# A two-layer cross-attention and expert network on one core: first experts on tokens sorted by expert, one batch behind the other, query and key stacks written from SBUF to SBUF

## The reference

```python
x = x + L0_xattn(layernorm(x), ctx)   # 16 heads of 8, softmax(q k / sqrt(8)) v, biases
x = x + L0_ffn(layernorm(x))          # 8 experts, 128 -> 512 -> 128, gelu, one expert a token
x = x + L1_xattn(layernorm(x), ctx)   # 16 query heads on 8 key heads, inputs quantised to 8 bit,
                                      # weights to -1, 0, 1; layernorm and requantising before Wo
x = x + L1_ffn(layernorm(x))          # 15 experts 128 -> 128 -> 128, relu, top 3 of a softmax,
                                      # and one shared expert
# L0_ffn:
idx = argmax(softmax(logits)); score = gates[idx]
h = gelu(x @ w1[e] + b1[e]); y = h @ w2[e] + b2[e]     # for every e
out = y[idx] * score
```

## Time and profile before

| what | value |
|---|---|
| runs, us | 273.32, 275.46, 277.76 (median 275.46) |
| span of the profiled execution, first to last instruction | 272.9 us |
| instructions | 4924 |
| PE busy | 225.1 us, 82% |
| DVE busy | 172.3 us, 63% |
| ACT busy | 140.1 us, 51% |
| POOL busy | 65.5 us, 24% |

### The profile page before, as it was taken

One profiled execution on the slowest core, in us unless ns is written; L12 is line 12 of the kernel. 1 busy time (PEld: TensorE's weight loads), 2 busy tenths in 40 slices (PEclk: granted clock), 3 DMA queues, 4 the chain that ended last, 5 costly groups with the idle time before them and its releaser, 6 DMA issues.

```text
span 272.9 us, 4924 instructions
## 1 busy us (share of the span) xinstructions
PE 225.1 (82%) x1700; PEld 141.5 (52%) x1700; DVE 172.3 (63%) x486; ACT 140.1 (51%) x329; POOL 65.5 (24%) x123
## 2 busy tenths in 40 slices
PE   2444697799898899999999985776997779979994
PEld 1323143434343379898899862222333233877893
DVE  7770697898793033232563588794898832887864
ACT  3411025688787763534454443723886386454551
POOL 6792059652295200100110000700000111111000
PEclk9999997999999999999999999577899798999999
DMA  6079013820058500000002000292000000000000
GB/s 176 13 133 222 13 30 107 251 53 17 3 164 214 155 2 0 1 4 0 2 0 68 21 0 1 70 269 59 0 4 1 2 0 2 1 0 2 19 4 19
DMA packets 10888, 14.36 MB, mean 53 GB/s; under 512 B 2698, under 2 KB 8512, under 8 KB 10672
## 3 DMA queue, kind: packets, MB, share of 16 engines
q1 hardware_dynamic: 7568, 6.92, 9.4%
q0 software_dynamic: 2528, 6.60, 9.2%
q10 hardware_dynamic: 768, 0.53, 0.7%
HBM read 11.73 MB, written 2.23 MB: 51 GB/s over the span
## 4 chain that ended last, share of the span: by engine, by line
PE 56%; DVE 14%; DMA 9%; POOL 6%; ACT 5%; SPq 5%; issue 4%; DVEq 0%; ACTq 0%; POOLq 0%
PE SB L1467 10%; PE OB L1402 9%; PE OB L1481 5%; DVE mx L1038 5%; PE SB L1513 5%; PE SA L1481 5%; PE SB L1382 4%; PE SA L1352 4%; PE SA L1524 4%; SPq L510 4%; DMA K<-k_dram 2%; ACT prob L798 2%; DMA k_dram<-kp 2%; DMA q_dram<-qp 2%; DMA wgn<-in_L_ffn_wg_dram 1%
## 5 line engine op out<-in xcount | busy, mean ns | idle before, releaser
L1038 DVE TENSOR_REDUCE mx<-SA 128x1 bf16<-128x512 f32 x128 | 79.9, 683 | 20.2 <-PE SA L1352 19.7
L798 ACT ACTIVATE prob<-SB 128x512 f32<-128x512 f32 x128 | 67.7, 598 | 25.9 <-PE SB L1382 25.3
L1352 PE MATMUL SA<-K,Q 64*128 64x512 bf16 x128 | 36.3, 441 | 14.3 <-DMA K<-k_dram 6.0
L1402 PE MATMUL OB<-prob,V 128*32 128x256 f32 x512 | 42.2, 416 | 1.7 <-ACT oT L806 1.5
L859 ACT ACTIVATE prob<-SB,b1T 128x256 f32<-128x256 f32 x64 | 26.7, 470 | 30.1 <-PE SB L1467 30.1
L1382 PE MATMUL SB<-Q,K 64*128 64x256 bf16 x256 | 31.9, 295 | 3.8 <-ACT prob L798 2.5
L633 POOL TENSOR_SCALAR vareps<-mv 128x2 f32<-128x2 f32 x10 | 1.9, 190 | 135.9 <-DVE mv L929 135.8
L1467 PE MATMUL SB<-hT,w1s 128*128 128x256 f32 x128 | 33.3, 385 | 0.6 <-ACT prob L859 0.6
L1352 PEld LDWEIGHTS SA<-K,Q 64*128 64x128 bf16 x128 | 9.4, 96 | 34.8 <-DVE mx L1038 19.2
L1467 PEld LDWEIGHTS SB<-hT,w1s 128*128 128x128 f32 x128 | 22.1, 190 | 3.8 <-ACT prob L859 1.5
L1382 PEld LDWEIGHTS SB<-Q,K 64*128 64x128 bf16 x256 | 12.0, 98 | 23.1 <-ACT prob L798 11.0
(11 more groups left out here) (249 smaller groups left out, 285.3 us busy)
## 6 DMA issues: line engine op xcount, KB each, us to landing
w1s<-in_L_ffn_w_dram POOLq DMA_DIRECT2D x8, 256.0 KB, 4.1
w2s<-in_L_ffn_w_dram POOLq DMA_DIRECT2D x8, 256.0 KB, 4.7
K<-k_dram SPq DMA_DIRECT2D x12, 128.0 KB, 5.2
Q<-q_dram SPq DMA_DIRECT2D x18, 64.0 KB, 2.2
e1w<-in_L_ffn_eW_dram POOLq DMA_DIRECT2D x1, 960.0 KB, 6.4
e2w<-in_L_ffn_eW_dram POOLq DMA_DIRECT2D x1, 960.0 KB, 7.9
q_dram<-qp SPq DMA_DIRECT2D x12, 64.0 KB, 1.7
k_dram<-kp SPq DMA_DIRECT2D x6, 128.0 KB, 1.8
```

What stands on the lines that cost most here:

```text
L798: act.activation(prob[:, g % 2, 2 * (i % 2) + a, 2 * u:2 * u + 2, :].rearrange("p k q -> p (k q)"), SB[n % 3][:, :], ACT.Exp).then_inc(s_e ...
L1038: dve.tensor_reduce(mx[:, g % 2, r, 2 * a + i // 2:2 * a + i // 2 + 1], SA[SCORE_BANK[n]][:, :], AX, ALU.max).then_inc(s_sa_max, 1)
L1352: pe.matmul(SA[SCORE_BANK[u]][:, :], Q[n][rows, b, p, r * P:(r + 1) * P], K[n][rows, b, key_group(n, p), :], start=True, stop=True).then_i ...
L1402: last = pe.matmul(OB[32 * j:32 * j + 32, 0:NQ], V[n][:, b, kt, first:first + 32], prob[:, gg % 2, j, kt, :], start=(kt == 0), stop=(kt == ...
```

## The change

- First experts. After the gate of a batch, count0, slots0 and tiles0 give every token a slot among 16 tiles of 32 slots, so that each tile holds tokens of one expert. gather0 multiplies the tokens by a 0/1 matrix (perm), 512 columns; permT0 makes its transpose. For each of four chunks of four tiles: weights0 copies each tile's expert weights (128x1024 f32) on POOL, at an address read from the computed table, into one of two chunk buffers; h0 is a bias product and four products of 32 rows by 512 columns side by side; ACT applies gelu to 128x512; gelT0 turns it; y0 is a bias product and sixteen products of 32 rows by 128 columns; scatter0 brings the outputs back to token order.
- Order. One list, written out. Batch 0's first experts follow layer 0's attention; then batch 0's queries of layer 1 and the scores of group 8; batch 1's first experts lie between the steps of groups 9 to 11; then batch 1's queries and the scores of group 12; batch 0's second experts lie between the steps of groups 14 and 15; batch 1's output turn to its last norm follow; then batch 1's second experts.
- Maxima. DVE turns them in 32x32 blocks; PE's two products and the copy are gone, and SP issues four transfers instead of two.
- Stacks. The parts go from kp and qp straight into K and Q, six transfers each, with no DRAM between them. Layer 1 uses layer 0's memory again.
- Banks. Two SA banks instead of three; two X banks in turn for all else, and the attention's banks once it has ended.

```diff
+elif kind == "weights0":                                            (gpsimd)
+    _, b, c = step
+    if c == 0:
+        pool.wait_ge(s_eid, b + 1)
+    before = nth(*step) - 3
+    if before >= 0:
+        pool.wait_ge(*xfull(("y0", before // CHUNKS, before % CHUNKS)))
+    for j in range(4):
+        place = pool.value_load(eid[0:1, b, 4 * c + j:4 * c + j + 1], min_val=0, max_val=E0 - 1)
+        pool.tensor_copy(wq[:, c % 2, j, :], w0s[:, bass.ds(place, 1), :].rearrange("p o f -> p (o f)")).then_inc(s_wq, 1)
...
+elif kind == "h0":                                                  (scalar)
+    act.activation(gel[:, c % 2, :], xbank(step)[:, :], ACT.Gelu).then_inc(xdone(step), 1)
...
+elif kind == "h0":                                                  (tensor)
+    pe.matmul(bank[:, :], owners[:, 4 * c:4 * c + 4, :].rearrange("e j s -> e (j s)"), b1s[:, :], start=True, stop=False)
+    for j in range(4):
+        pe.wait_ge(s_wq, 4 * nth("weights0", b, c) - 3 + j)
+        at = c * P + 32 * j
+        last = pe.matmul(bank[32 * j:32 * j + 32, :], xs[:, at:at + 32], wq[:, c % 2, j, 0:F0], start=False, stop=True)
...
+elif kind == "y0":                                                  (tensor)
+    pe.wait_ge(*xread("gelT0", b, c))
+    pe.matmul(bank[:, 0:D], owners[:, 4 * c:4 * c + 4, :].rearrange("e j s -> e (j s)"), b2r[:, :], start=True, stop=False)
+    for k in range(FC):
+        for j in range(4):
+            last = pe.matmul(bank[32 * j:32 * j + 32, 0:D], gelT[:, c % 2, k * P + 32 * j:k * P + 32 * j + 32],
+                             wq[:, c % 2, j, at:at + D], start=False, stop=(k == FC - 1))
...
+dve.transpose(nm[:, g % 2, :, :, :].rearrange("p x c r -> p x r c"), mx[:, g % 2, :, :, :]).then_inc(s_nm, 1)
...
-sp.dma_start(dram[part].rearrange("e s c -> (e s) c"), parts[:, part, :]).then_inc(written[part], 16)
+engine.dma_start(K[n][b][row:P:8, :, :], kp[0:P // (n + 1), u, part, :]).then_inc(s_kst[n][b], 16)
...
 SCHEDULE (batch 0's experts; the handovers)
+('weights0', 0, 0), ('weights0', 0, 1), ('h0', 0, 0), ('gelT0', 0, 0), ('h0', 0, 1), ('y0', 0, 0), ('weights0', 0, 2),
+('gelT0', 0, 1), ('h0', 0, 2), ('y0', 0, 1), ('weights0', 0, 3), ('out_turn', 0, 1, 0), ('gelT0', 0, 2), ...
+('scatter0', 0), ('turn', 'f0', 1), ('stats', 'q1', 0), ('red0', 1), ('norm', 'q1', 0), ('logits0', 1), ('quant', 'q1', 0),
+('gate_exp0', 1), ('turn', 'q1', 0), ('count0', 1), ('qproj', 1, 0), ('slots0', 1), ('qstack', 1, 0), ('scores', 8, 0),
+('scores', 8, 1), ('scores', 8, 2), ('scores', 8, 3), ('max_rows', 8), ('scores', 9, 0), ('scores', 9, 1),
+('scores', 9, 2), ('exp', 8, 0), ...
```

More of the change, by code:

```diff
@@ L237 @@
-SCHEDULE = build_schedule()
-def between(step):
-    at = SCHEDULE.index(step)
-    return any(SCHEDULE.index(("exp", 8 * n, 0)) < at < SCHEDULE.index(("exp", 8 * n + 7, 3)) for n in range(2))
-X_WANT = {
-    "ctxq_turn": lambda s: [s[1]], "kproj": lambda s: [0], "vproj": lambda s: [1] if s[1] else [],
-    "turn": lambda s: [int(s[1] == "q0")],
-    "qproj": lambda s: [1], "bias_turn": lambda s: [0], "w1_measure": lambda s: [1],
-    "w1_turn": lambda s: [1], "wg_turn": lambda s: [0], "out_turn": lambda s: [s[3]], "att_turn": lambda s: [0],
-    "out_proj": lambda s: [1], "red0": lambda s: [0], "logits0": lambda s: [1],
-    "max_rows": lambda s: [0], "bias0": lambda s: [0, 1], "logits1": lambda s: [1], "bias1": lambda s: [0, 1],
-}
@@ new lines, with place_banks @@
+X_USES = {"ctxq_turn": 1, "kproj": 1, "vproj": 1, "turn": 1, "qproj": 1, "bias_turn": 1, "w1_measure": 1, "w1_turn": 1,
+          "wg_turn": 1, "out_turn": 1, "att_turn": 1, "out_proj": 1, "red0": 1, "logits0": 1, "count0": 1, "slots0": 1,
+          "tiles0": 1, "gather0": 1, "permT0": 1, "h0": 1, "gelT0": 1, "y0": 1, "scatter0": 1, "logits1": 1, "bias1": 2,
+          "hidden1": 1, "output1": 1}
+def place_banks():
+    banks, counts, last, used = {}, {}, {}, [0] * (3 + NSA + NSB)
+    for at, step in enumerate(SCHEDULE):
+        uses = X_USES.get(step[0], 0)
+        if not uses:
+            continue
+        free = [0, 1]
+        if at > SCHEDULE.index(("scores", 15, 3)):
+            free += list(range(2, 2 + NSA))
+        if at > SCHEDULE.index(("exp", 15, 3)):
+            free += list(range(2 + NSA, 2 + NSA + NSB))
+        if at > SCHEDULE.index(("values", 15, 3)):
+            free += [2 + NSA + NSB]
+        banks[step] = []
+        for k in range(uses):
+            bank = min(free, key=lambda x: last.get(x, -1))
+            last[bank] = at + 0.5 * k
+            used[bank] += 1
+            banks[step].append(bank)
+            counts[step, k] = used[bank]
+    return banks, counts
@@ L289 @@
+X_BANKS, X_COUNT = place_banks()
+OUTPUTS_BEFORE = {("bias1", b): sum(s[0] == "output1" for s in SCHEDULE[:SCHEDULE.index(("bias1", b))]) for b in range(B)}
 ORDER = {}
@@ L487, in xread, with turned, columns, buffer_free @@
             return x_read[X_BANKS[step][k]], X_COUNT[step, k]
+        def turned(bank, stage):
+            return bank[:, 0:NQ] if stage[0] != "q" else bank[:, 0:NQ].rearrange("d (r p) -> d p r", r=R)
+        def columns(stage, b):
+            return hT[:, b, :] if stage[0] != "q" else hT[:, b, :].rearrange("d (p r) -> d p r", r=R)
+        def buffer_free(engine, step):
+            kind, b = step[:2]
+            if b and kind == "gather0":
+                engine.wait_ge(*xfull(("h0", b - 1, CHUNKS - 1)))
+            elif b and kind in ("permT0", "y0"):
+                engine.wait_ge(*xfull(("scatter0", b - 1)))
         def split_group(g):
@@ L818, in _ @@
                     last.then_inc(s_sq, 1)
-                elif kind in ("turn", "att_turn", "red0", "bias0", "bias1") and step in ON_SCALAR:
+                elif kind in ("turn", "att_turn", "red0", "bias1", "gather0", "permT0", "gelT0", "y0") and step in ON_SCALAR:
                     b = step[-1]
@@ L822, in _ @@
                     if kind == "turn":
-                        last = act.activation(hT[:, b, :], xbank(step)[:, 0:NQ], ACT.Copy)
+                        last = act.activation(columns(step[1], b), turned(xbank(step), step[1]), ACT.Copy)
                     elif kind == "att_turn" and step[1] == 0:
@@ L1308, in _ @@
                     _, n, b = step
+                    fill(step)
                     if n == 0:
@@ L1443, in _ @@
                     last.then_inc(xfull(step)[0], 1)
-                elif kind == "bias0":
+                elif kind == "count0":
+                    b = step[1]
+                    fill(step)
+                    pe.wait_ge(s_place, 4)
+                    pe.wait_ge(s_cw, CW_AT["logits0", b])
+                    for r in range(R):
+                        last = pe.matmul(xbank(step)[0:E0, 0:1], oh_b[:, r, :], ones_b[:, 0:1], start=(r == 0), stop=(r == R - 1))
+                    last.then_inc(xfull(step)[0], 1)
+                elif kind == "slots0":
                     b = step[1]
```

847 lines of the change are left out of this document (362 added, 485 removed), and 33 rows, old and new, of tables (ON_SCALAR, SCHEDULE).

## The result

The changed kernel takes 338.5 us (median of 4 runs, 336.42 to 340.32), the kernel before 276.4 in the same comparison (273.32 to 277.76): a ratio of 1.229 with a 95% interval of 1.217 to 1.240. Forecast were 294 us with a range of 276 to 312. The direction was right, the size was wrong by 44 us.

A forecast was written before the change was run, and what follows sets the result against it. The prediction took the kernel as PE-bound where work lies beside a chain, latency-bound elsewhere. Stages 35.5 + 57 + 32.5 + 26 + 46 + 28 + 33 + 14.5 + 19.6 gave 292 us of span; forecast 294, range 276 to 312.

The forecast's parts named there:

- Layer 0's attention: First exponentials to the end of layer 0's attention with slots known: 57 us, ending at 92.5 us.
- 51, at the 0.89 of now 57 us: Layer 0's attention: PE's 46.3 us lose 2, take in 2.8 and 3.8, divided by the present busy share.
- Two SA banks instead of three cost nothing: Layer 0's attention: no cost from one score bank fewer, bound 0 to 4 us.
- Groups 12 to 15: Layer 1, batch 1: 18.3 plus twelve second experts at 0.88 plus logits 1 gives 30, at 0.9: 33 us.
- 5.2 a group: Layer 1's attention: PE work per group; four groups less the scores already made take 18.3 us.
- Groups 8 to 11 with batch 1's experts: Layer 1, batch 0 mixed with batch 1's first experts: 39 us plus 7.5 of waits, 46 (40 to 55).
- The last chain: Batch 1's output turn through quantising to its last norm and turn: 14.5 us, filled only by four leftover experts.
- Batch 0's first experts: Stage paced by POOL's weight copies, 1.25 us a tile, taking turns with products: about 33 us, 32.5 in the sum.
- Handovers and start: Handovers to layer 1's groups 8 and 12 take 26 and 28 us; first exponential at 35.5 us.
- Rival 1: Whole kernel: PE's work decides and it gets faster, 257 us of span, 260 of time; chance 0.11.
- Rival 2: Whole kernel: shorter chains and POOL copies at 1.0 us leave no change, 275 us; chance 0.13.
- Rival 3: Whole kernel: table read of 0.8 us adds 10 and 5, low clock adds 4: 313 us; chance 0.16.

The follow-up runs named there:

- a_kst32: Changed kernel with three SA and two SB banks and both layer-1 key stacks issued behind shift 7: 331.2 us.
- a_lead32: Changed kernel with three SA, two SB banks, layer 0's scores and maxima one exp step earlier, second key stack behind shift 7: 321.7 us.
- a_late: Changed kernel with batch 0's second experts behind all of attention, batch 1's output chain between them: 324.7 us, ratio 1.173.
- the merged lists: Changed kernel, batch 1's first experts in first handover and group 8, no second handover, batch 0's second experts behind attention: 325.9 us; with three SA, two SB banks 319.0.

## Why the prediction was wrong, and where it was right

**Layer 0's attention: 57 forecast, 73.9 measured, the largest miss.** The step that failed is the sum of PE's work, "51, at the 0.89 of now 57 us". PE's records fill 61.8 us of the window at 0.85 of it, and the clock there is 0.77 instead of 0.98. The sum took for granted that the list feeds PE as the old one did. It doesn't: its scores and maxima stand one exp step later, and its shift has four issues instead of two on a queue shared with the stacks. The lead is the large part: one exp step earlier takes the first copy of weights from 106.0 (a_kst32) to 98.5 us (a_lead32), and first to eighth group from 58.2 to 50.9. The banks are a small one: "Two SA banks instead of three cost nothing while a PE step (1.3) is as long as two reductions of DVE (2 x 0.62); bound 0 to 4" put at nothing what costs 2.5 us to the eighth group in the changed order, within its own bound, and 7.8 in the old one, outside it. The reductions alone would fit, but DVE has 45.1 us of work in the 73, and its other operations now reach PE more often. The queue costs the groups nothing here (95.3 and 95.2); it cost them in the old order. Undoing the banks, the queue and the lead brings the stage, first exponential to first copy of weights, from 74.5 us to 61.7 (a_lead32): 12.8 of 17 are accounted for by parts, about 2 of these by the clock behind the eighth group. The rest isn't, but one piece of it is in the trace: the slot chain, from the gate's first copy at 103.5 to the first copy of weights at 112.3, takes 8.8 us where 7 were taken. I had counted the turned maxima as a saving on PE and named SP's four issues only for the first exponentials and the handovers.

**Groups 12 to 15: 33 forecast, 39.5 measured.** The step that failed is "5.2 a group (46.3/8 less max_rows and projections)", divided by a busy share of 0.9 as if a group were work and not a cadence. For the four groups and the logits the sum thus has 19.3/0.9 = 21.4 us; in a_late, without experts between them, they take 28.0. The trace before had the cadence already: 44.0 us from the first to the eighth group, 6.3 each, and 31.1 from group 12's first exponential to group 15's last values, with batch 0's output chain between them, in this window:

```profile
202.00:233.50 31.50, 26.18 (x267) 10.85 (x263) 19.43 (x63) 20.12 (x48) 2.66 (x6) 0.89 0.01 1
```

Of the 6.6 us the experts gave 2.2 back (9.5 measured, 12 x 0.88/0.9 = 11.7 taken), and 2.0 from the stage's start to ACT's first exponential, a load of its table with them, were in no term. Why a bare group takes 7.0 is shown in part only: waits, the one for group 15's shift above all, and a clock of 0.72, not told apart.

**Groups 8 to 11 with batch 1's experts: 46 forecast, 54.7 measured.** The term that failed is PE's work, put at 39 us with 7.5 of waits on top; PE's records fill 49.5 of 55 us. ACT, put at 33 us, is busy for 32.3. Why PE's part is so much larger stays open. The first 11 us of the stage run at half clock, and behind the exponentials of the four groups, which end at 203.7 us, 21.8 us follow in which copies and products of the last chunks take turns, as in batch 0. No run changes this stage's parts one at a time, and these groups aren't bare, so a_late's 7.0 can't be carried over.

**The last chain: 14.5 forecast, 20.7 measured.** The chain itself is 16.7 us (295.5 to 312.2): 10.0 to the end of quantising, where 9.4 was taken, and 6.8 behind it, where 5.4 was; the other 4 us are leftover experts of batch 0, which I counted as filling under the chain, while the list has them ahead of its first link.

**Batch 0's first experts: right in kind, 34.9 for 32.5.** Three bursts of copies, the wait for y0 and the order of the turns came as forecast. The copy was overrated, 1.25 us against 1.0 (eight in 7.91, the table's read with nothing to be seen), which should have given 4 us back; the products took it: at the stage's start gather is at half clock (3.63 us for four records; 1.98 in batch 1, at full clock), and h0 of chunk 2 is drawn out to 3.9 us by its copies. The Trainium skill, GPSIMD Engine Reference, section 3.1, would have an element in 1.03 cycles at 1.2 GHz, by my estimate from that page 0.88 us plus start for a copy; the trace's 1.037 us agrees, with 0.16 left for the start. The Trainium skill, ScalarE: Activation LUTs, section "What ACT_TABLE_LOAD costs", adds a drain of 1.38 us to a switch; the trace doesn't show it, and it was rightly left out of the sum.

**Handovers and start: right.** 24.6 and 26.5 for 26 and 28; the first exponentials come at 37.4 for 35.5. Of the prediction's own signs, PE under 30% busy in the handovers did not come (11.7 of 25 us and 12.2 of 26, records at half clock), and one that it had named as wrong did: PE over 80% busy between 92 and 225 us, 31.2 of 35 and 49.5 of 55.

**The rivals.** Rival 1 (PE's work decides) fell: PE's busy share is 75%. Rival 2's quick copies were there, and gained nothing. Rival 3 (313 us) had the direction and came nearest. Its larger term, the table's read, is nothing; its smaller one, 4 us for the clock behind idle stretches, is about what the runs show: 1.2 and 1.1 in the handovers and 2.7 behind the eighth group. The sum itself had no term for round trips; each stage was one engine's busy time over a share borrowed from a stage with other company.

The parts apart, for the whole kernel: direct stacks gain 6 us; turned maxima cost 5.5 on top of them in the old order, most of it by the stacks' place in SP's queue; two score banks cost 4.4 in the changed order, 10.7 in the old one and 7 with the merged lists; the place of batch 0's second experts costs 14. Whether sorted tiles in place of dense experts would gain in the old order, with batch 1's end of attention and the handovers laid under them, was not tried and stays open. The best kernel found is the one before with direct stacks and the key stacks issued behind the last shift: 267.7 us, where the kernel before takes 280.3.
